# Cross-attention and a binarised feed-forward layer on one core: values blocks 4 to 7, two key weight blocks and the second constants made in the scores' bank, and every engine's list reordered

## The reference

```python
def _L0_xattn_ref(query, key, value, mask, Wq, Wk, Wv, wq_h, bq_h, wk_h, bk_h, wv_h, bv_h, Wo):
    qh = jnp.einsum('bsd,dh->bsh', q, wq_h) + bq_h
    kh = jnp.einsum('bsd,dh->bsh', k, wk_h) + bk_h
    vh = jnp.einsum('bsd,dh->bsh', v, wv_h) + bv_h
    scores = jnp.einsum('bsh,bth->bst', qh, kh) / jnp.sqrt(jnp.float32(HD))
    scores = jnp.where(mask, jnp.float32(-1000000000.0), scores)
    attn = jax.nn.softmax(scores, axis=-1)
    out_h = jnp.einsum('bst,bth->bsh', attn, vh)
    out = jnp.tile(out_h, (1, 1, H))
    return jnp.einsum('bsd,de->bse', out, Wo)
...
x = x + _L0_xattn_ref(_layernorm(x, axis=-1), ctx_1024, ctx_1024, mask_SxS2_bk1, ...)
x = x + _L0_ffn_ref(_layernorm(x, axis=-1), ...)
```

## Time and profile before

| what | us |
|---|---|
| median of 3 runs | 328.83 (328.49 to 330.87) |
| the profiled execution | 327.9 |
| its span | 326.1 |
| busy: PE, ACT, DVE, POOL | 301.0, 270.1, 265.9, 234.9 |

### The profile page before, as it was taken

How to read it: one execution, slowest core, us unless ns; L and a number is a source line. 1 busy time by engine, 2 the same in 40 slices (tenths; PEclk the granted TensorE clock), 3 DMA queues, 4 the chain that set the end, 5 groups by cost and what they waited for, 6 DMA issues and landing times.

```text
span 326.1 us, 6210 instructions
## 1 busy us (share of the span) xinstructions
PE 301.0 (92%) x2055; PEld 204.9 (63%) x2055; DVE 265.9 (82%) x589; ACT 270.1 (83%) x444; POOL 234.9 (72%) x396
## 2 busy tenths in 40 slices
PE   5899789749999999999999999999999999999994
PEld 4635557425777676667666766676677666667773
DVE  3699997888899997999799979987896759657353
ACT  1048867398999989998999999999999999898760
POOL 2480795867698999999989998995748556584431
PEclk9996555787999999999999999999999999999999
DMA  7795527945563768466736572546061505233211
GB/s 230 245 384 120 128 49 148 194 113 97 63 148 54 173 110 219 58 165 125 202 59 159 141 194 51 94 118 161 16 144 36 131 16 131 46 103 80 115 65 64
DMA packets 85184, 40.34 MB, mean 124 GB/s; under 512 B 77464, under 2 KB 80672, under 8 KB 85152
## 3 DMA queue, kind: packets, MB, share of 16 engines
q1 hardware_dynamic: 84240, 39.90, 50.7%
q10 hardware_dynamic: 912, 0.05, 0.2%
HBM read 12.80 MB, written 8.39 MB: 65 GB/s over the span
## 4 chain that ended last, share of the span: by engine, by line
PE 46%; POOL 18%; ACT 16%; DVE 9%; issue 5%; DMA 3%; SPq 0%; ACTq 0%; POOLq 0%; DVEq 0%
PE psZ L1416 18%; PE psY L1401 18%; POOL xh L490 7%; ACT psY L625 5%; POOL x1b L514 3%; PE psY L1302 3%; ACT magnitudes L606 3%; POOL rstd L479 3%; ACT h_hi L634 3%; POOL w_sb L525 3%; DMA ctx_sb<-in_ctx 2%; PE psW L1357 2%; PE psW L1377 2%; ACT L625 2%; DVE st_raw L766 2%
## 5 line engine op out<-in xcount | busy, mean ns | idle before, releaser
L1416 PE MATMUL psZ<-sgn2T,h_hi 128*128 128x256 f16 x512 | 114.2, 273 | 0.4
L1416 PE MATMUL psZ<-sgn2T,h_lo 128*128 128x256 f16 x512 | 114.2, 273 | 0.0
L899 DVE SCALAR_TENSOR_TENSOR h_lo<-psY,h_scale,h_hi 128x1024 f16<-128x1024 f32 x64 | 81.7, 1279 | 35.1 <-ACT h_hi L634 34.8
L1401 PE MATMUL psY<-xT_hi,sgn1T 128*128 128x512 f16 x256 | 98.0, 383 | 7.2 <-DVE h_lo L899 6.1
L1401 PE MATMUL psY<-xT_lo,sgn1T 128*128 128x512 f16 x256 | 98.0, 383 | 0.0
L625 ACT ACTIVATE psY<-psY,b_col,alpha1x 128x512 f32<-128x512 f32 x128 | 91.3, 745 | 6.6 <-PE psY L1401 5.6
L634 ACT ACTIVATE h_hi<-psY,h_scale 128x1024 f16<-128x1024 f32 x64 | 71.3, 1114 | 5.7
L525 POOL TENSOR_TENSOR w_sb<-w_sb,x1b 128x256 f32<-128x256 f32 x62 | 43.1, 729 | 38.1 <-DVE w_sb L913 38.1
L1416 PEld LDWEIGHTS psZ<-sgn2T,h_hi 128*128 128x128 f16 x512 | 50.1, 98 | 10.7 <-issue 2.1
L1416 PEld LDWEIGHTS psZ<-sgn2T,h_lo 128*128 128x128 f16 x512 | 50.1, 98 | 8.6
L514 POOL TENSOR_TENSOR x1b<-x,b_bc 128x256 f32<-128x256 f32 x64 | 54.0, 874 | 2.0
(11 more groups left out here) (160 smaller groups left out, 434.1 us busy)
## 6 DMA issues: line engine op xcount, KB each, us to landing
out_x<-w_sb SPq DMA_DIRECT2D x15, 512.0 KB, 3.0
x_in<-in_x SPq DMA_DIRECT2D x4, 512.0 KB, 4.2
ctx_sb<-in_x SPq DMA_DIRECT2D x4, 512.0 KB, 4.4
w_sb<-in_L_ffn_w SPq DMA_DIRECT2D x2, 1024.0 KB, 8.1
wkq<-in_x SPq DMA_DIRECT2D x4, 512.0 KB, 6.2
ctx_sb<-in_ctx SPq DMA_DIRECT2D x1, 1024.0 KB, 7.7
wvv<-in_x SPq DMA_DIRECT2D x2, 512.0 KB, 4.6
vh_tile<-in_x SPq DMA_DIRECT2D x2, 512.0 KB, 4.7
```

Of the source, the lines that this page charges most:

```text
L899: nc.vector.scalar_tensor_tensor(out=h_lo[q][:, :, :], in0=psY[q % 2][:, :, :], scalar=h_scale[:, :], in1=h_hi[q][:, :, :], op0=ALU.mult, ...
L1401: last = nc.tensor.matmul(psY[q % 2][:, c % 2, :], sgn1T[:, c, k, :], part[b % 2][:, :, k, :], start=(n == 0), stop=(n == 2 * KD - 1))
L1416: last = nc.tensor.matmul(Z[n][:, (j % 2) * D:(j % 2 + 1) * D].rearrange("p (k t) -> p k t", k=KD), part[q][:, u, j * P:(j + 1) * P], sgn2 ...
```

## The change

**What moves.** Six blocks are made in steps 0 to 5 and one, M(2), at the end of the head, all in psW0, the bank of the scores: the table LATE says after which batch's scores. late(b) stands in the lists of PE, ACT and DVE; PE's waits until scores(b) has read psW0, and score(b+1) waits until the block has been copied out (wait_late_read). The first values blocks use Y[0] to Y[3] once each.

```diff
             return not 0 <= b < B
 
 
-        V_bank = [Y[n % 4] for n in range(B // 2)]
-        M_bank = [Y[2], Y[3], Y[2], Y[3]]
+        V_bank = [Y[n] if n < 4 else W[0] for n in range(B // 2)]
+        M_bank = [Y[2], Y[3], W[0], W[0]]
+        C_bank = [Y[0], W[0]]
+
...
+        LATE = {3: ("M", 2), 4: ("M", 3), 5: ("C", 1), 6: ("V", 4), 7: ("V", 5), 8: ("V", 6), 9: ("V", 7)}
+
+        def wait_late_read(eng, b):
+
+            if b - 1 not in LATE:
+                return
+            kind, n = LATE[b - 1]
+            if kind == "M":
+                eng.wait_ge(M_copied, n + 1)
+            elif kind == "C":
+                eng.wait_ge(c_copied, n + 1)
+            else:
+                eng.wait_ge(V_copied, n + 1)
 
         @block.sync
...
 
             def values(n):
 
-                if n < 2:
-                    pe.wait_ge(c_copied, n + 1)
+                if n == 0:
+                    pe.wait_ge(c_copied, 1)
+                elif n == 1:
+                    pe.wait_ge(kv_maxed, NH)
+                    pe.wait_ge(khT_copied, NH)
                 elif n < 4:
-                    pe.wait_ge(M_copied, n + 1)
-                else:
-                    pe.wait_ge(V_copied, n - 3)
-                pe.wait_ge(vhT_copied, 2 if n < B // 4 else 4)
+                    pe.wait_ge(M_copied, n - 1)
+                pe.wait_ge(vhT_copied, 2 if n == 0 else 4)
                 for m in range(2):
                     last = nc.tensor.matmul(V_bank[n][:, m * D:(m + 1) * D],
                                             vhT[V_AT:, 2 * n + m, :, :].rearrange("p h t -> p (h t)"),
                                             wo_sum[V_AT:, :], start=True, stop=True)
                 last.then_inc(pe_V, 1)
+
+            def late(b):
+
+                if b not in LATE:
+                    return
+                pe.wait_ge(sc_steps, val(b, 3, 2))
+                kind, n = LATE[b]
+                if kind == "M":
+                    score_weights(n // KD, n % KD)
+                elif kind == "C":
+                    score_constants(n)
+                else:
+                    values(n)
 
             def sum_alpha2():
...
@@ -1351,6 +1395,7 @@
                 wait_turned(pe, (pe_turned_lo[0], KD), lo_turned[0][b % 2], b)
 
                 wait(pe, sc_steps, val(b - 1, 3, 2))
+                wait_late_read(pe, b)
                 for j in range(T):
                     for n, (k, part) in enumerate((k, part) for k in range(KD)
```

**The order of the steps.** On every engine the steps are rearranged: scores are now computed five batches ahead instead of four, and PE's step ends a group earlier (first_product(b-1, 7) opens the next). PE's and ACT's:

```diff
             def step(b):
+                first_product(b - 1, 7)
                 second_product(b - 1, 0)
                 second_product(b - 1, 1)
                 first_product(b, 0)
                 first_product(b, 1)
-                score(b + 4)
+                late(b + 4)
                 first_product(b, 2)
                 first_product(b, 3)
                 second_product(b - 1, 2)
                 attend(b + 2, 0)
                 second_product(b - 1, 3)
+                score(b + 5)
                 first_product(b, 4)
                 first_product(b, 5)
                 attend(b + 2, 1)
                 first_product(b, 6)
-                first_product(b, 7)
...
             def step(b):
+                gelu(b - 1, 2)
+                gelu(b - 1, 3)
+                round_h(b - 1, 1)
+                exp(b + 3)
+                round_e(b + 2)
+                round_x(b, 1)
+                gelu(b - 1, 4)
                 gelu(b - 1, 5)
                 round_h(b - 1, 2)
                 gelu(b - 1, 6)
                 gelu(b - 1, 7)
                 round_h(b - 1, 3)
-                round_e(b + 2)
+                round_x(b + 5, 0)
                 squares(b + 1)
-                round_x(b + 6, 0)
                 gelu(b, 0)
                 gelu(b, 1)
+                late(b + 4)
                 round_h(b, 0)
-                gelu(b, 2)
-                gelu(b, 3)
-                round_h(b, 1)
-                round_x(b + 1, 1)
-                exp(b + 4)
-                gelu(b, 4)
```

268 lines of the change are left out of this document (137 added, 131 removed).

## The result

The kernel takes 330.3 us after the change (median of 20 runs, 328.11 to 331.54), against 329.14 us for the kernel before in the same session (325.72 to 332.48). The ratio is 1.0049, 95% interval 1.0033 to 1.0066: half a per cent slower, within what I had called no change. The forecast was 324.2 us, a gain of 4.6; the time lies inside its range (319.5 to 330.5), at the very edge. Medians are of all executions, while the ratios compare fast executions only (those more than 1.5% above the fastest of their kernel are left out), so the two can differ by some tenths of a per cent.

The account below looks back on a forecast made before the run. PE was taken as the bound after a 61.8 us head, with ACT also nearly full until 210 us. Terms: -6.9 + 0.6 + 2.6 - 0.9 + 0 = -4.6 us, giving 324.2 us; range 319.5 to 330.5.

Parts of the forecast that it names:

- Term 2: Steps 1 to 5: each block adds 0.95 us to PE's step, 16.61 against 16.18; with packing +2.6 us.
- Term 4: Pipeline steps: the new order of work costs nothing, xT_lo's transpose being covered by 1.5 us; 0, bounds -1.6 and +10.
- term 3: PE-bound end: score(4) runs in the head, so one step less there holds a score; -0.9 us.
- slower rival: Steps with an exp: low half of xT(b+1) comes too late for the first product; +10.5 us, 334.5; chance 0.13.
- Term 1: Head: work leaves it, so the first gelu comes at 62.5 instead of 69.44 us; -6.9 us.
- the mean of batch 0, 49.2: Head, on DVE: the mean of batch 0 comes at 49.2 instead of 50.05 us, a gain of 0.9.
- the lower bound of -2.9: Head: if ACT's old delay is kept, only the first product's 2.9 us is gained.
- packing: Steps with blocks: work never packs perfectly, so +0.5 us beyond PE's own +2.1.
- Given back in the steps: Steps 1 to 8 run at about 16.9 us, giving 4 us of the start's gain back: 328; chance 0.15.
- It does more: Head gains 8.4 instead of 6.9 us and steps 6 to 8 fall to 15.66: -7.7, 321.1; chance 0.17.
- The clock rival: Step 0: PE's clock stays at half through it, costing +2.2 us, 326.4; chance 0.10.
- The rule that I weighed: Head: by the rule, less matmul work and more gaps could leave PE at the low clock longer.

Follow-up runs that it names:

- run 3: The kernel before in its own orders, with only the six blocks moved from the head into steps 0 to 5: 327.4 us, ratio 0.996.
- run 2: The kernel before with the same six blocks left out of its head, later batches reading earlier ones: 324.96 us, ratio 0.9901.
- run 12: The kernel before with the six blocks in steps 0 to 5 and, in step 0, ACT's first gelus ahead of squares and round_x: 329.1 us, ratio 1.0006.
- run 13: The kernel before in its own order, six blocks made in steps 0, 2, 4, 6, 8 and 10 instead of the head: 328.37 us, ratio 0.9946.
- run 7: The changed kernel with exponentials from batch 4 on computed with the gelu's table, so no table loads in the steps: 327.47 us, ratio 0.9954.
- run 1: The changed kernel with the six blocks left out of the steps and made nowhere: 327.47 us, ratio 0.9977.
- run 6: The changed kernel with half of POOL's addition of the residual to the output left out: 329.36 us, ratio 1.002.

## Why the prediction was wrong

By the mean account, -4.6 became about +1.7. Steps 1 to 10 cost 5.5 us where terms 2 and 4 had 2.6: this is the step that failed most. Of the 5.5, the blocks are 3.5 (run 3 against before) and the new order, which I had put at nothing, 2.0 (the changed kernel against run 3). The head gave 3.9 where I had 6.3, and the 0.9 of term 3 came to nothing. That the time is inside the range is luck: the range reached up to 330.5 for the sake of the slower rival, whose mechanism the changed kernel's trace doesn't show, and the half per cent was lost in another way.

**Term 1, the head (-6.9, in step 0 +0.6, so -6.3 at step 1).** Right in kind: ACT's wait of 3.21 us for the mean of batch 1 is gone. The size failed at the first link, "the mean of batch 0, 49.2": I took half of DVE's freed time as gain, but the chain didn't run through DVE's work there. It ran from the scores of batch 3 (done 50.07; I had 47.3) through the block of M(2) on PE and its copy on ACT, which now stands ahead of the squares of batch 0. The mean of batch 0, which stands behind those scores on DVE, was late by 2.6 us against mine, the squares waited 1.0 more for M(2)'s copy, and the first product was late by 2.8, at 61.70. Measured at step 1: -5.74 in the first pair, -2.87 in the second, about -3.9 in the mean. Of this, leaving the blocks out of the head gives most by itself: runs 2, 3, 12 and 13, with the head's order of before, begin step 1 at 74.37, 75.70, 77.57 and 76.63, 1.7 to 4.9 us before 79.2. I had taken the value "since it is followed step by step", but each link assumed that the one before was the last to end; the lower bound of -2.9 (-2.3 at step 1) was nearer to -3.9 than the value.

**Term 2, blocks in the steps (+2.6).** Two of its numbers erred in the same direction. The base: "against 16.18", an average over steps 1 to 8, where steps 1 to 5 were on average 15.95 with four of them at 15.66 to 15.73 (in the second profile of before 16.11, so this part of the error is between 0.4 and 1.15 us). The block: "take 0.95", measured 1.16 as it stands between others. The floor is thus 5 x 16.82 = 84.1 instead of 5 x 16.61 = 83.1, and the base 79.75 or 80.53 instead of 80.9: +4.4 or +3.6 where I had +2.1. For "packing" I had +0.5, measured +1.0 (85.08 against 84.11), which goes with less work on ACT alone (run 7, 84.19). Together +5.3 or +4.6 in steps 1 to 5. In the old order (run 3) these steps cost 4.3 against the mean of before, and steps 6 to 10, shorter by 0.8, gave some back: 3.5.

**Term 3 (-0.9).** It came and brought nothing. The step without scores came one earlier, step 11 at 14.77 instead of 15.66, as forecast; step 12 was then 15.80 instead of 14.81, where PE waited 0.7 us in two places for DVE's `h_lo`. What was saved in one step was lost in the next, in both profiles.

**Term 4, the new order (0).** It costs: +3.6 us over ten steps without blocks (runs 1 and 2), +2.0 with them. In the changed kernel not by the mechanism of my slower rival. That one wanted PE to wait for the transposed `xT_lo`; in its steps 1 to 10 the waits of PE that the trace shows are these (us in total, times, longest):

```profile
PE psY L1446 <- DVE h_lo L924: 1.5, 3, 0.8
PE psW L1422 <- DMA eT<-e_hl: 1.3, 2, 1.0
PE psW L1402 <- issue: 0.9, 1, 0.9
```

In run 3, the old order with blocks, only this; and in run 1, the new order without blocks, the four below it:

```profile
PE psY L1447 <- DVE h_lo L921: 1.5, 2, 0.8
```
```profile
PE psY L1442 <- DVE h_lo L922: 2.9, 4, 1.4
PE psW L1418 <- DMA eT<-e_hl: 2.7, 2, 1.4
PE psY L1442 <- DMA xT_lo<-w_sb: 1.1, 1, 1.1
PE psW L1398 <- issue: 0.9, 1, 0.9
```

So what is new with the order are waits before the attend for the transpose of e, and one before the score, for which the trace names no cause: together 2.2 us in the changed kernel, about as much as it is longer than run 3. Run 1 waits 7.6 us in all, run 2 3.0, for a difference of 3.6; once, for 1.1 us, it is the `xT_lo` of my slower rival. By their size these waits account for the cost, roughly; no run moved e's transpose back alone to show it. All but 0.2 us of the changed kernel's waits lie in steps 6 to 10.

A second thing is visible: DVE and POOL take longer for some of their work. POOL's addition of the residual takes 1044 ns in steps 1 to 5, beside 731 ns before, and DVE's masking 948 ns beside 480 (in the second pair 1047 beside 725, and 878 beside 415). Other work of POOL got shorter: a normalisation of `x_in` takes 555 ns beside 805.

```profile
L540 POOL TENSOR_TENSOR w_sb<-w_sb,x1b 128x256 f32<-128x256 f32 x18 | 18.3, 1044 | 0.0
...
L863 DVE COPY_PREDICATED sc<-mask_sb,masked_sb 128x256 f32<-128x256 uint8 x6 | 5.7, 948 | 0.0
```
```profile
L525 POOL TENSOR_TENSOR w_sb<-w_sb,x1b 128x256 f32<-128x256 f32 x16 | 11.1, 731 | 0.0
...
L838 DVE COPY_PREDICATED sc<-mask_sb,masked_sb 128x256 f32<-128x256 uint8 x5 | 2.4, 480 | 0.0
```

Less work on POOL (run 6) bought nothing in steps 1 to 5 and 1.5 us in steps 6 to 10; but less on ACT bought 1.4 there too (run 7), so neither engine is shown to pace them alone. How the rest of the order's cost divides over its moves wasn't tried: they were not undone one by one.

**The rivals.** "Given back in the steps" was the right one: 328, at 0.15, with steps 1 to 8 at 16.9. Measured are steps 1 to 5 at 17.0 and steps 6 to 8 at 16.5, 16.8 over all eight. I had argued against it that PE "is there already full and only waited 0.5 a step"; a full PE is the very reason that a block costs its whole length. "It does more" failed in both halves: the head gave 5.7 and 2.9 instead of 8.4, and steps 6 to 8 took 16.5 a step, not 15.66. (The slower rival's 334.5 is mis-added: 324.2 and 10.5 make 334.7.) The clock rival was right as a mechanism, at up to 1.6 us rather than 2.2, but I treated it as a state of the kernel, while it differs from one execution to the next, and it meets the kernel before as well.

**The rule that I weighed.** By the Trainium skill, "TensorE: Matmul & The Clock Gate", section "Part 1: The HAM clock gate", the clock is throttled by default and PE activity releases it. The runs say no more than the earlier trace rows did: PE was busy 9.87 of 10 us from 40 to 50 us in the changed kernel at a granted clock of 0.50, and in two executions of one kernel it rose 3 and 7 us into the same work. What the clock is granted for in this head stays open.

**What beats both.** Moving the blocks alone, in the old order, gives 0.996 (0.9933 to 0.9988), and one in every second step 0.9946 (0.9906 to 0.9986): 1.3 and 1.8 us off 329 us, and the only versions computing the whole that are faster than before with an interval below 1. By the medians the two are 0.9 and 0.5 us faster, so the gain is small and the two can't be told apart. Of the change as it stands, the new order of the steps is the part that costs without a return.

## What to carry to other kernels

Moving work out of a latency-bound head into a pipeline that one engine fills is a trade, not a gain: the head gives back what lay on its chain, the pipeline charges the full length of what was put in for each step that this engine paces. Price it against the single steps in their sequence, since an average over steps can hide that most are already at the floor (15.66 here, with an average of 16.18), and take the price of an instruction from where it stands between others (start of the one before to start of the one after), not in a row of its kind. Where several engines are nearly full, relieving one may buy only the distance to the next: here 0.8 to 0.9 us of 85 for TensorE or ScalarE, and 0.1 to 0.3 for the other two. And read a head from more than one profile: here two executions of one kernel began step 1 2.7 us apart, where the change itself gains 3.9 in the mean.

## What was not expected of the hardware

After the head TensorE's clock fell once more to its lower level around the first product, in six of eight profiles with the changed kernel's head, and for how long differs between executions of the same kernel: about 3 us in one profile and 7 us in the other. Starting the first gelu earlier need not help: run 12 had its first gelu 3.3 us before run 3's and its step 1 1.9 us after it, with the clock at 0.50 instead of 1.00 from 66 to 70 us. A two-pass fp32 product over 16 rows and 512 columns costs 1.16 us between fp16 matmuls at the full clock, where the eight-matmul group of such work at the low clock gave 1.89 a block. POOL's addition of 128 x 256 fp32 took 731 ns on average in one order of the steps and 1044 ns in another (878 with the blocks left out), DVE's masking 480 and 948 ns, with no change to either instruction. Why isn't shown.
